# New order tables for score products, maxima and exponentials in a nine-part transformer kernel, and four instead of two row buffers for its routed experts

## What is computed

```python
x = _layernorm(x + _L0_attn_ref(...)); x = _layernorm(x + _L0_ffn_ref(...))
x = _layernorm(x + _L1_attn_ref(...)); x = _layernorm(x + _L1_ffn_ref(...))    # 16 heads; 8 experts, top 2, one shared
x = _layernorm(x + _L2_attn_ref(...)); x = _layernorm(x + _L2_ffn_ref(...))    # causal, rotary; GQA and 8 experts, top 2
x = _layernorm(x + _L3_attn_ref(...)); x = _layernorm(x + _L3_ffn_ref(...))    # causal, ALiBi; GELU feed-forward
# each attention:  scores = q k^T * scale (+ mask or bias);  attn = softmax(scores);  out = attn v
```

## Time and profile before

| | us |
|---|---|
| median of 3 runs | 1179.25 |
| lowest, highest | 1177.85, 1180.4 |
| the profiled execution, its whole time | 1175.86 |
| its span, first to last instruction | 1174.0 |

### The profile page before, as it was taken

The page is one execution under the profiler, slowest core; times in us unless marked ns, Lnnn a source line. Parts: engine busy times, 40 slices in busy tenths (PEclk is TensorE's granted clock), DMA queues, the critical chain, the costliest instruction groups (busy, mean ns, idle before and its releaser), DMA issues.

```text
span 1174.0 us, 25534 instructions
## 1 busy us (share of the span) xinstructions
PE 1011.7 (86%) x8024; PEld 486.2 (41%) x8024; DVE 836.2 (71%) x2567; ACT 671.8 (57%) x1361; POOL 404.4 (34%) x675
## 2 busy tenths in 40 slices
PE   3479898888889988979999999898989787999986
PEld 1312232322256664334444444443556333444355
DVE  5998889787535556778888888774333677788666
ACT  2207777764745442547667777566555264777652
POOL 5623243223323632534324322334235452331121
PEclk8659999997989998889999999989999778999999
DMA  6123443421012332212212412111233321121001
GB/s 158 37 77 136 152 151 109 162 81 33 28 55 66 92 104 67 89 50 83 86 54 64 166 41 64 62 37 38 62 97 107 90 72 34 57 66 34 2 1 37
DMA packets 85628, 88.10 MB, mean 75 GB/s; under 512 B 13100, under 2 KB 72204, under 8 KB 85304
## 3 DMA queue, kind: packets, MB, share of 16 engines
q1 hardware_dynamic: 69149, 71.90, 19.6%
q0 software_dynamic: 4160, 8.53, 2.6%
q10 hardware_dynamic: 12187, 6.05, 1.8%
HBM read 45.41 MB, written 40.11 MB: 73 GB/s over the span
## 4 chain that ended last, share of the span: by engine, by line
PE 55%; issue 17%; DVE 12%; ACT 7%; POOL 4%; DVEq 2%; DMA 1%; POOLq 1%; SPq 0%; ACTq 0%
PE bank L2469 13%; PE bank L2455 7%; PE bank L2430 6%; PE bank L2439 5%; PE bank L2405 4%; ACT PT L1439 4%; DVE M L1863 3%; DVE masked_scores L1860 3%; PE bank L2715 3%; PE bank L2689 3%; PE bank L2693 2%; PE bank L2490 1%; PE bank L2700 1%; POOL slots_x L1244 1%; PE bank L2401 1%
## 5 line engine op out<-in xcount | busy, mean ns | idle before, releaser
L1439 ACT ACTIVATE PT<-bank 128x512 f32<-128x512 f32 (+2 forms) x832 | 414.1, 543 | 213.2 <-PE bank L2455 159.0
L1863 DVE TENSOR_REDUCE M<-bank 128x1 f32<-128x512 f32 (+1 forms) x448 | 258.5, 627 | 51.8 <-PE bank L2430 48.8
L2455 PE MATMUL bank<-QS,KS 64*128 64x512 bf16 (+3 forms) x1024 | 236.0, 329 | 23.3 <-ACT PT L1439 20.3
L2430 PE MATMUL bank<-KS,QS 61*128 61x512 bf16 (+3 forms) x1024 | 241.6, 343 | 16.8 <-DVE M L1860 9.0
L1860 DVE CUSTOM_DVE_ANT_0 masked_scores<-bank,maskw 128x384 bf16<-128x384 f32 (+1 forms) x384 | 219.4, 621 | 47.5 <-PE bank L2430 44.7
L2469 PE MATMUL bank<-PT,VA 128*32 128x512 f32 (+3 forms) x2048 | 225.1, 513 | 2.0 <-ACT PT L1439 1.6
L2439 PE MATMUL bank<-half_ident,half_mask 64*128 64x64 bf16 (+1 forms) x1536 | 152.2, 212 | 21.9 <-ACT PT L1439 13.5
L2439 PEld LDWEIGHTS bank<-half_ident,half_mask 64*128 64x128 bf16 x1536 | 78.8, 96 | 149.2 <-ACT PT L1439 82.0
L2430 PEld LDWEIGHTS bank<-KS,QS 61*128 61x128 bf16 x1024 | 77.7, 98 | 117.0 <-DVE M L1863 45.1
L2455 PEld LDWEIGHTS bank<-QS,KS 64*128 64x128 bf16 x1024 | 74.9, 96 | 82.8 <-ACT PT L1439 62.5
L1128 POOL CAST MS<-M 128x16 bf16<-128x16 f32 x64 | 14.0, 219 | 229.2 <-DVE M L1863 229.2
(11 more groups left out here) (307 smaller groups left out, 1474.1 us busy)
## 6 DMA issues: line engine op xcount, KB each, us to landing
QS<-scr_q SPq DMA_DIRECT2D x128, 96.0 KB, 2.3
slots_x<-XSB SPq DMA_DIRECT2D x32, 256.0 KB, 2.6
scr_q<-PQ SPq DMA_DIRECT2D x16, 384.0 KB, 2.4
KS<-scr_k SPq DMA_DIRECT2D x64, 96.0 KB, 2.4
XSB<-slots_x SPq DMA_DIRECT2D x92, 64.0 KB
slots_y<-YSB ACTq DMA_DIRECT2D x20, 256.0 KB, 2.5
scr_q<-PQ SPq DMA_DIRECT2D x16, 256.0 KB, 2.7
MW<-in_m_w SPq DMA_DIRECT2D x9, 392.0 KB
```

The lines of the kernel that those rows point to most:

```text
L1439: a.activation(PT[kt % 2][:, js[0]:js[-1] + 1, q0:T], tiles(bank[st_bank(L, g, i)][:, 0:w * len(js)], len(js)), ACT.Exp, scale=LAYERS[L][" ...
L1863: v.tensor_reduce(M[g % 2][:, t * GH + js[0]:t * GH + js[-1] + 1], tiles(src[:, 0:kl * len(js)], len(js)), AX_X, ALU.max, negate=True).the ...
L2430: r = mm(to[:, n * kl:(n + 1) * kl], QS[rows_of(j, ROWS_SHIFT), q_slot(g, j), t * P:(t + 1) * P], KS[rows_of(j, ROWS_SHIFT), kv_slot(L, g, ...
L2455: r = mm(to[:, n * w:(n + 1) * w], KS[rows_of(j), kv_slot(L, g, j), kt * P:(kt + 1) * P], QS[rows_of(j), q_slot(g, j), T - w:T], start=not ...
```

## The change

The three tables are replaced by others of the same form. The same number of Ts, Ss, maxima and exponentials stands in them; no other code of the attentions is altered. Beside that, the number of row buffers becomes a constant with the value 4, and what counted modulo 2 counts modulo 4.

```diff
 SCORE_ORDER = {
-    0: ["TTS STT SSS - TTSSS SS TTSS T T SS S T T TT ST TS", "SS TTS ST TS SSS TST T TS SS TTS S TT TS ST T TS", ...
+    0: ["STT TS SST TSSS - STTS TS S T T TS TT SS TST T SS", "T SS TST SST TS TSS S ST TS STTS TT ST ST TT T S", ...
...
 REDUCES_AT = {
-    0: ["1121121120012001", "1111211111201011", "1122122201101111", "2010111111110001",
+    0: ["1111111120000011", "2121221212201001", "1112121201101101", "1111112230000011",
...
 EXPS_AT = {
-    0: ["1111022011111111", "1101111111111111", "1112201111111110", "1111101111101111",
+    0: ["1111114010101010", "1111211111111111", "1112111111111111", "2222200101010101",
...
+XS_BUFS = 4
+
+
 def rows_landed(rq):

     counts = [x[3] for x in QUAD if x[1] is not None]
-    return 16 * sum(counts[j] for j in range(rq % 2, rq + 1, 2))
+    return 16 * sum(counts[j] for j in range(rq % XS_BUFS, rq + 1, XS_BUFS))
...
-        XSB = [sb(f"XSB{i}", [P, NT, P]) for i in range(2)]
+        XSB = [sb(f"XSB{i}", [P, NT, P]) for i in range(XS_BUFS)]
...
-        xs_landed = [sem(f"dma_xs{i}") for i in range(2)]
+        xs_landed = [sem(f"dma_xs{i}") for i in range(XS_BUFS)]
...
-                    at_least(sp, xs_t, rq - 1)
+                    at_least(sp, xs_t, rq + 1 - XS_BUFS)
                     for j in range(n):
                         row = sp.value_load(row_at[0:1, group, at + j:at + j + 1], min_val=0, max_val=(E * GROUP_TILES - 1) * P)
-                        sp.dma_start(XSB[rq % 2][:, j, :], slots_x[group][bass.ds(row, P), :]).then_inc(xs_landed[rq % 2], 16)
+                        sp.dma_start(XSB[rq % XS_BUFS][:, j, :], slots_x[group][bass.ds(row, P), :]).then_inc(xs_landed[rq % XS_BUFS], 16)
...
                 def slots_t(q):
                     rq = ROUTED_NO[q]
-                    pe.wait_ge(xs_landed[rq % 2], rows_landed(rq))
+                    pe.wait_ge(xs_landed[rq % XS_BUFS], rows_landed(rq))
                     at_least(pe, xst_ready, rq)
                     for i in range(QUAD[q][3]):
-                        r = tr(bank[5][:, i * P:(i + 1) * P], XSB[rq % 2][:, i, :], ident[:, :])
+                        r = tr(bank[5][:, i * P:(i + 1) * P], XSB[rq % XS_BUFS][:, i, :], ident[:, :])
```

More of the change, by code:

```diff
@@ new lines @@
+    1: ["012341200100", "101120111111", "212112121212", "122000001121",
+        "200230100111", "011110000100", "101011560000", "000022222222",
+        "212001210111", "011110000100", "101111550010", "010112221222",
+        "200121210110", "110110000100", "101011560010", "010112221222"],
+    2: ["211111110111", "011110000010", "001011550111", "111111212121",
+        "211011100111", "111110101011", "011223230111", "111111111111",
+        "111012200111", "011110030312", "203011110111", "111111111100",
+        "012230121220", "001110000101", "010010010000", "000000000000"],
@@ L201 @@
+    3: ["222223000000", "001113111212", "122121221111", "120000101111",
+        "111111230101", "010111200100", "101222120101", "010111211211",
+        "211212230101", "010110001010", "101111440101", "010112121212",
+        "121212120010", "101010011111", "120000000000", "000000000000"],
 }
 EXPS_AT = {
-    0: ["1111022011111111", "1101111111111111", "1112201111111110", "1111101111101111",
-        "1123213000101111", "1111111211211211", "2112201101100101", "0010133301100010",
-        "0123213010101111", "0111101101111111", "1112411111112111", "1111201101111111",
-        "1112211111101011", "0101101111111111", "1111501111110111", "1111111111111111"],
@@ L216 @@
-    3: ["001152300000", "000001111111", "111201111121", "111121221220",
-        "111122200010", "111110110111", "011101111121", "111122220110",
-        "111122201011", "111110110111", "011121111121", "111121110111",
-        "111111121120", "111110111111", "111122220111", "111101111111"],
+    0: ["1111114010101010", "1111211111111111", "1112111111111111", "2222200101010101",
+        "0111260000011111", "1111211121112111", "2112101101101101", "1011111201101111",
+        "1111224010111111", "1111101010111112", "1112011121112111", "2111201101101110",
+        "1111311111111112", "1111201101101101", "1011611111110111", "1101111110111111"],
@@ new lines @@
+    1: ["121220112211", "111120000010", "000141121121", "121120110111",
+        "111201201200", "111110101101", "101161111111", "111110110111",
+        "011160011200", "110110110111", "011141111121", "111120111111",
+        "111140101201", "111110111111", "111111111111", "111120110111"],
+    2: ["011160101200", "111111111111", "111121111111", "111111220101",
+        "010151100200", "110110111111", "111141111111", "111111120101",
+        "010161100200", "111110111101", "111111111121", "111121120101",
+        "101131111120", "111111111111", "111120111111", "111111111111"],
@@ L220 @@
+    3: ["003301201111", "111110101010", "101161111111", "111120111110",
+        "111123300000", "111111111111", "111101111121", "111122220010",
+        "011123300000", "110111111111", "111120111111", "111112330010",
+        "010131111111", "111110111111", "111140110111", "111101111111"],
 }
```

26 lines of the change are left out of this document (3 added, 23 removed), and 48 rows, old and new, of the table SCORE_ORDER.

## The result

The changed kernel takes 1136.34 us (median of 4 runs, 1131.25 to 1137.08) where the kernel before takes 1179.83 beside it: 0.9623 times as long, 95% interval 0.9592 to 0.9655. The profiled execution took 1137.08 us with a span of 1135.2.

The account below looks back on a forecast made before the run. It took attentions 1 to 3 as filled by TensorE, and attention 0 as three nearly full engines, none the only limit. Terms -3.5 - 6.5 + 2.8 + 1.2 = -6.0 us gave 1173.2 us from 1179.25; range 1159 to 1188.

Parts of the forecast that it names:

- (a): Layers 0 and 3: products in opposite halves run together, saving column passes at 0.21 us each; -3.5 us.
- (b): Layer 0: fewer Ss held behind Ts that wait for exponentials, so VectorE waits less for scores; -6.5 us.
- it hides nothing that could come out: 0: Layers 1 to 3: bunches of Ss are thinned too, but TensorE is 95 to 97% busy there; 0.
- (c): Layer 0: 7 bursts now come closer behind their exponentials, with only one further T issued; +2.8 us.
- (d): TensorE's runs of S and T rise from 353 to 364, each end costing up to 0.1 us; +1.2 us.
- (e): ScalarE's writes of turned maxima and query projection stand behind more exponentials, but these free their Ts earlier; 0.
- (f): Four row buffers: loads come earlier, but TensorE waits for no row DMA, so nobody gains; 0.
- VectorE's takeover: Rival, layer 0: Ss always come in time, VectorE's whole wait goes and pairing counts in full; 1161.8 us, chance 0.14.
- ScalarE's pacing: Rival: exponentials set the pace of Ts, freed TensorE time becomes waits; about 1179 to 1181 us, chance 0.15.
- The late bursts: Rival, layer 0: bursts with one T of lead stand 1.17 us each and the clock falls; 1189.2 us, chance 0.25.

Follow-up runs that it names:

- Ts first: The changed kernel with all Ts of an item ahead of its Ss, same number of both at every item; 1163.99 us, ratio 0.980 to the kernel before.
- e4: The kernel before with four row buffers and its old tables; ratio 0.997 to the kernel before.
- e8: The changed kernel with two row buffers instead of four; 1136.59 us, ratio 0.959 to the kernel before.
- e12: The kernel before with four maxima in block 0 group 3 of layers 1 and 3 moved behind the routed block's norm; ratio 0.993.
- e6: The kernel before with 20 unused matmuls on TensorE ahead of the turned inputs of block 3 in layers 1 and 3; ratio 0.992.
- e9: The kernel before with all Ss of an item ahead of its Ts in layer 0 alone; ratio 1.000 to the kernel before.

## Why the prediction was wrong, point by point

The sign was right and the size was a seventh of what came, with the wrong causes.

**(a) Pairing, -3.5.** Refuted as a cause by itself. Ts first keeps every paired pass in layer 0 and loses 2.6 of the 3.6 us of the first five units, so pairing without the order is worth at most the other 1.0. The term priced a saved pass at 0.21 us wherever TensorE is the chain, though three engines were nearly full.

**(b) Held Ss, -6.5.** The mechanism is half of one. VectorE's wait fell to 12.2, not under 10. On the old tables, Ss ahead cost 1.4 us in five units (73.8 for 72.4): ScalarE's wait for Ts rose there from 12.9 to 14.9 us, and VectorE's for Ss rose too, from 8.3 to 9.4, where (b) had it fall. The prediction priced one side of an exchange.

**(b) again, "it hides nothing that could come out: 0" for layers 1 to 3.** This is the step that failed most. It took TensorE's 95 to 97% busy for a bound. The busy time then shrank by 3.5 us in layer 3, with as many matmuls, and by 2.7 in the middle stage beside the clock's 1.3. In layer 3 most of that can be passes saved by pairing, since Ts first has it too; in the middle stage, where the prediction's count of passes hardly moves, what the busy time held is not shown. The Trainium skill (Perfetto Trace Analysis, Identifying the Most-Contended Engine) says that matmul busy time is no good measure of how close TensorE is to its limit and that the share of LDWEIGHTS is a better one. The trace agrees with the first half. The loads' share was 45% in the middle stage (93.25 of 205) and is 45% now (91.50 of 202); it had left room where the busy share seemed to leave none, but no run here shows that it measures the room. I had not applied this. Here stood 8.3 us in two stages, 7.0 without the clock's part.

**(c) and (d), +2.8 and +1.2.** No sign of (c): up to the start of layer 0's last unit the queue stood 1.1 us at bursts for exponentials, and 0.8 before. (d) was not isolated, and stays open; it is under what these runs can tell.

**(e) and (f), 0.** (f) is right: e4 and e8. (e) was not tested.

**The stretches chosen.** What the sum left out altogether is the joins. I read windows from inside the attentions, which is where work repeats; but 26 of the 38.8 us lie outside such stretches. Both stands of TensorE, 5.11 and 6.16 us, stood in the trace of before with a falling clock behind them, and no term spoke of them. e12 shows that four maxima made some 4 of the 7.3 and 9.0 us by which these units got shorter, e6 that about 2.5 us of each such unit come through the clock. And no term priced the clock's rise, which by the estimate above is some 10 us in all.

**The rivals.** VectorE's takeover (1161.8) was nearest in size, but its condition isn't met: in 95 to 240 VectorE still waits 12.2 us for Ss. ScalarE's pacing is seen in the 44.2 us at Ts, but as a cost and not as a stop. The late bursts didn't come. That rival set lower shares of ScalarE and VectorE beside the low clock; what bears on the clock is e6, where only TensorE was given more to do. What was named as proof against the prediction, that attentions 1 and 2 move by more than 3 us and that the clock's dips shift, is what came: layers 1 and 2 gave 12.5 us, and slices of the clock row changed.

**Stays open:** what made the 9 us of layer 0's second half, beside the clock (0.92 to 0.97). One unit of it, block 2 group 3, holds 5.6 of them (20.4 to 14.7 us, clock 0.75 to 1.00), and ScalarE's waits for bursts fell in layer 0. Up to the start of its last unit, before (94 to 319 us):

```profile
ACT PT L1439 <- PE bank L2469: 14.5, 7, 5.4
```

and changed (93 to 306 us):

```profile
ACT PT L1442 <- PE bank L2472: 4.4, 4, 1.9
```

The longest, 5.4 us, lies in that unit and ends at 271.9 us: exponentials there wait until a burst has freed their part of PT, and the burst stood behind Ss that waited for maxima. No term of the prediction and no run of mine took up this wait. Open too is which rows of the new tables matter most; the exponentials' table was never changed alone. In the steady stages the order of products and the place of the maxima only work together, so their shares can't be added.

## What to carry to other kernels

Measure each stage of a hand-ordered program from a repeated mark to the next, joins included, before choosing where to read; then take each stand of the fullest engine over 1 us and ask what the other engine did just before. An engine that takes work early in a line that runs in order isn't ahead: it makes whoever needs its next other step wait, and four maxima in the wrong place cost 4 us. Don't take a high busy share of TensorE for a floor.

## What the runs showed of the hardware

Where the granted clock is full, the seven units of layer 0 and the stage of layer 3 repeat to 0.1 us across chips; only one unit of the middle stage took 8.5 us in some runs and 9.2 in others at a full clock. Most of a kernel's scatter is in stretches with a lower clock. On one chip the kernel before took 1177.25 us at a mean clock of 0.921 and 1193.26 at 0.904. On another it took 1260 at 0.88. In e9 and e12, which ran there with the experts' code untouched, the stage with experts 1 took 189 and 188 us at a clock of 0.86 and 0.84, instead of 158 at 0.92. How much of that is the clock, and why chips differ by 7%, the runs don't say.
